# Copied patches written in four strips, images read in halves, and the second part of each group's patches read from GpSimd's queue

## What is computed

```python
xn   = (x - mean(x, (2, 3))) / sqrt(var(x, (2, 3)) + 1e-5)
pat  = patchify(pad(xn, to=40), 8)                  # 32*25 patches, 32 x 10 x 10
log  = pat.mean((2, 3)) @ Wg + bg
r    = one_hot(argmax(log), 8) * softmax(log)
y    = einsum('ne,encij->ncij', r, [relu(conv3x3(pat, Wexp[e]) + bexp[e]) for e in range(8)])
out  = x + unpatchify(y)[..., :32, :32]
```

## Time and profile before

| | before |
|---|---|
| median of three runs | 229.51 us (228.51 to 230.57) |
| the profiled execution's own time | 225.47 us |
| its span, first to last instruction | 223.7 us |
| busy: PE / PE weight load / DVE / ACT / POOL | 174.3 / 151.8 / 162.6 / 127.8 / 8.7 us |
| mean granted TensorE clock | 0.88 of full speed |
| SP's queue | 58,844 packets, 35.54 MB, 59.9% of 16 DMA engines |
| DMA packets under 512 bytes | 53,898 of 59,326 |
| instruction queue q8 | 44 packets, 0.72 MB |

### The profile page before, as it was taken

One profiled execution on the slowest core, in us unless ns is written; L12 is line 12 of the kernel. 1 busy time (PEld: TensorE's weight loads), 2 busy tenths in 40 slices (PEclk: granted clock), 3 DMA queues, 4 the chain that ended last, 5 costly groups with the idle time before them and its releaser, 6 DMA issues.

```text
span 223.7 us, 12210 instructions
## 1 busy us (share of the span) xinstructions
PE 174.3 (78%) x5652; PEld 151.8 (68%) x5652; DVE 162.6 (73%) x367; ACT 127.8 (57%) x239; POOL 8.7 (4%) x10
## 2 busy tenths in 40 slices
PE   0198769998599969898699749894999977997730
PEld 0038658887488858687597648784888866896730
DVE  4796997995997549975997619990799758078145
ACT  3235527594796319971996366571498587786000
POOL 7700000000000000000000000000000000000000
PEclk9999995699979976999699955999569999997995
DMA  6784975599369474958496836955795488001002
GB/s 224 180 240 108 220 173 218 133 211 273 133 130 233 131 278 108 214 155 317 94 216 170 312 84 140 254 191 186 169 232 225 123 173 210 6 6 71 32 3 94
DMA packets 59326, 37.28 MB, mean 167 GB/s; under 512 B 53898, under 2 KB 54794, under 8 KB 58378
## 3 DMA queue, kind: packets, MB, share of 16 engines
q1 hardware_dynamic: 58844, 35.54, 59.9%
q10 hardware_dynamic: 432, 0.97, 1.2%
HBM read 21.62 MB, written 14.43 MB: 161 GB/s over the span
## 4 chain that ended last, share of the span: by engine, by line
PE 50%; DMA 13%; DVE 13%; issue 10%; SPq 9%; ACT 4%; DVEq 0%
PE conv_bank L551 33%; PE chunk_bank L540 14%; SPq L213 8%; DMA windows<-WIND 6%; DMA XT<-x 5%; ACT XG L470 2%; DMA out<-XT 2%; DVE ROWS L324 2%; DVE STATS L297 1%; DVE XN L312 1%; DVE WS L398 1%; PE chunk_bank L525 1%; DVE XG L371 1%; ACT WS L465 1%; DVE BLK L384 1%
## 5 line engine op out<-in xcount | busy, mean ns | idle before, releaser
L551 PE MATMUL conv_bank<-XG,WS 97*32 97x64 f32 x4800 | 114.7, 248 | 27.2 <-issue 24.4
L551 PEld LDWEIGHTS conv_bank<-XG,WS 97*32 97x32 f32 x4800 | 98.2, 155 | 37.1 <-issue 28.7
L465 ACT COPY WS<-chunk_bank 97x500 f32<-97x500 f32 (+1 forms) x150 | 76.1, 566 | 24.3 <-PE chunk_bank L540 22.8
L540 PE MATMUL chunk_bank<-HOTT,WPF 128*128 128x100 bf16 x768 | 53.8, 225 | 2.5 <-ACT WS L465 1.0
L540 PEld LDWEIGHTS chunk_bank<-HOTT,WPF 128*128 128x128 bf16 x768 | 41.8, 107 | 9.6 <-issue 3.3
L470 ACT COPY XG<-XG 32x1400 f32<-32x1400 f32 (+1 forms) x48 | 41.3, 861 | 7.5 <-DMA XG<-windows 6.7
L378 DVE STREAM_TRANSPOSE YT<-conv_bank 128x320 f32<-128x320 f32 x40 | 19.9, 508 | 24.6 <-PE conv_bank L551 24.3
L371 DVE COPY XG<-XG 32x1400 f32<-32x1400 f32 (+1 forms) x32 | 18.1, 567 | 0.7
L384 DVE STREAM_TRANSPOSE BLK<-YT 128x1024 f32<-128x1024 f32 x8 | 17.3, 2167 | 0.1
L324 DVE TENSOR_REDUCE ROWS<-XN 128x165 f32<-128x1650 f32 x8 | 14.7, 1841 | 0.1
L297 DVE BATCH_NORM_STATS2 STATS<-XT 128x6 f32<-128x512 f32 x16 | 10.3, 681 | 5.4 <-DMA XT<-x 5.4
(11 more groups left out here) (41 smaller groups left out, 79.6 us busy)
## 6 DMA issues: line engine op xcount, KB each, us to landing
XG<-windows SPq DMA_DIRECT2D x64, 150.0 KB, 3.5
windows<-WIND SPq DMA_DIRECT2D x7, 1250.0 KB, 7.1
XG<-windows SPq DMA_DIRECT2D x64, 100.0 KB, 2.4
out<-XT SPq DMA_DIRECT2D x16, 256.0 KB, 3.5
XT<-x SPq DMA_DIRECT2D x7, 512.0 KB, 5.3
windows<-WIND SPq DMA_DIRECT2D x3, 250.0 KB, 3.3
XT<-x SPq DMA_DIRECT2D x2, 256.0 KB, 4.5
windows<-WIND SPq DMA_DIRECT2D x1, 500.0 KB, 5.7
```

What stands on the lines that cost most here:

```text
L465: nc.scalar.copy(to, source).then_inc(chunk_copied, 1)
L540: last = nc.tensor.matmul(chunk_bank[c % NCB][:, j * GN:(j + 1) * GN], wide(co, kx), HOTT[:], start=True, stop=True)
L551: last = nc.tensor.matmul(o, WS[g % 2][0:KC, kx * C:(kx + 1) * C, patch], taps, start=kx == 0, stop=kx == TAPS - 1)
```

## The change

Five edits, all in the issuing of transfers and the waits on them:

1. `write_windows(g)` now calls `write_strip(g, v)` for all four strips and every group: rows of 2000 bytes three times, and of 4000 bytes once, where one transfer had rows of 10,000. VectorE's four window copies of a group each signal `strip_ready` in place of one signal behind all of them.
2. `load_x` reads each image group in two halves (256 KB each).
3. `read_patches` on SP issues part 0 only (8 transfers). Part 1 is issued by GpSimd, in a loop over the groups at the end of its list, behind a wait for the written windows.
4. GpSimd's second subtraction of the weights also waits for `normalised`.
5. ScalarE loads its activation table before it issues the loads of constants and gates.

```diff
         def x_arrived(g):
-            return x_loaded[g % XB], 16 * (g // XB + (g % XB > 0))
+            return x_loaded[g % XB], 32 * (g // XB + (g % XB > 0))
         def writes_done(g):
-            return 16 * (KEEP + g)
+            return 16 * KEEP * (g + 1)
...
+        def read_part(queue, g, part):
+            u, (lo, hi) = g % 2, PART_LOTS[part]
+            if g > 1:
+                queue.wait_ge(conv_done, LOTS * (g - 2) + hi)
+            for b in range(GI):
+                some = slice(b * NP + lo * LOT, b * NP + hi * LOT)
+                for ky in (0, 2):
+                    queue.dma_start(XG[u][ky * C:(ky + 1) * C, some],
+                                    windows_dram[u].rearrange("(n j) w -> j n w", j=C)
+                                    [:, some, ky * WIN:ky * WIN + KROWS]
+                                    ).then_inc(part_loaded[u][part], 16)
...
             def load_x(g):
-                sp.dma_start(XT[g % XB][:], x_rows[g]).then_inc(x_loaded[g % XB], 16)
+                for h in range(2):
+                    half = slice(h * HALF, (h + 1) * HALF)
+                    sp.dma_start(XT[g % XB][:, half], x_rows[g][:, half]
+                                 ).then_inc(half_loaded[h] if g == 0 else x_loaded[g % XB], 16)
...
+            def write_strip(g, v):
+                u, last = g % 2, NP if v == KEEP - 1 else (v + 1) * NB
+                if g > 1 and v == 0:
                     for part in range(2):
                         sp.wait_ge(part_loaded[u][part], 16 * READS * (g // 2))
-                sp.dma_start(windows_dram[u].rearrange("(p k) w -> p (k w)", k=NP), WIND[:]
-                             ).then_inc(windows_written, 16)
+                sp.wait_ge(strip_ready, g * KEEP + v + 1)
+                sp.dma_start(windows_dram[u].rearrange("(p k) w -> p k w", k=NP)[:, v * NB:last, :],
...
+            def write_windows(g):
+                for v in range(KEEP):
+                    write_strip(g, v)
             def read_patches(g):
                 sp.wait_ge(windows_written, writes_done(g))
-                for part, (lo, hi) in enumerate(PART_LOTS):
...
+                read_part(sp, g, 0)
...
             for part in range(PARTS - 1):
                 pool.wait_ge(part_ready, part + 1)
+                if part == 1:
+                    pool.wait_ge(normalised, 1)
                 nc.gpsimd.tensor_tensor(W0, W0, WPART[:, part, :], ALU.subtract).then_inc(rest_ready, 1)
...
+            for g in range(GROUPS):
+                if g == 1:
+                    pool.wait_ge(wp_loaded, 16 * PARTS)
+                pool.wait_ge(windows_written, writes_done(g))
+                read_part(pool, g, 1)
...
             act.dma_start(W0, weights).then_inc(w_loaded, 16)
+            nc.scalar.preload_act_table_set("natural_log_exp_and_others")
             act.dma_start(CONST[:], consts).then_inc(const_loaded, 16)
             act.dma_start(GATE[:], gates).then_inc(gate_loaded, 16)
-            nc.scalar.preload_act_table_set("natural_log_exp_and_others")
```

More of the change, by code:

```diff
@@ L124, in build @@
         normalised = sem("normalised")
-        strip_ready, windows_ready, windows_written = sem("strip_ready"), sem("windows_ready"), sem("windows_written")
+        strip_ready, windows_written = sem("strip_ready"), sem("windows_written")
         share_ready = sem("share_ready")
@@ L152, in x_arrived @@
         def x_arrived(g):
-            return x_loaded[g % XB], 16 * (g // XB + (g % XB > 0))
-        def windows_copied(g):
-            return (windows_ready, g) if g > 0 else (strip_ready, KEEP)
+            return x_loaded[g % XB], 32 * (g // XB + (g % XB > 0))
         def writes_done(g):
-            return 16 * (KEEP + g)
+            return 16 * KEEP * (g + 1)
         def weights_of(g, c):
@@ L201, in write_strip @@
                              WIND[:, v * NB * WIN * WIN:last * WIN * WIN].rearrange("p (k w) -> p k w", w=WIN * WIN)
                              ).then_inc(windows_written, 16)
+            def write_windows(g):
+                for v in range(KEEP):
+                    write_strip(g, v)
             def read_patches(g):
-                u = g % 2
                 sp.wait_ge(windows_written, writes_done(g))
-                for part, (lo, hi) in enumerate(PART_LOTS):
[L208 to L216, removed]
+                read_part(sp, g, 0)
@@ L232, in set_ones @@
                 sp.dma_start(XG[u][TAPS * C:KC].rearrange("p n k -> p (n k)"), ones).then_inc(ones_set[u], 16)
-            for h in range(2):
-                sp.dma_start(XT[0][:, h * HALF:(h + 1) * HALF],
-                             x_rows[0][:, h * HALF:(h + 1) * HALF]).then_inc(half_loaded[h], 16)
+            load_x(0)
             set_ones(0)
@@ L240, in _ @@
             spread(1)
-            write_strip(0)
+            write_strip(0, 0)
             spread(2)
             for v in range(1, KEEP):
-                write_strip(v)
+                write_strip(0, v)
             read_patches(0)
@@ L309, in normalise @@
                 if g > 0:
-                    dve.wait_ge(*windows_copied(g - 1))
+                    dve.wait_ge(strip_ready, KEEP * g)
                 inside = bass.AP(XN, PITCH + 1, [[PITCH * PITCH, 128], [PITCH, H], [1, W]])
@@ L318, in windows @@
                 dve.wait_ge(windows_written, writes_done(g - 1))
-                for to, source in window_copies():
-                    last = nc.vector.tensor_copy(to, source)
-                last.then_inc(windows_ready, 1)
+                copies = window_copies()
+                for to, source in copies[:2]:
+                    nc.vector.tensor_copy(to, source)
+                for to, source in copies[2:]:
+                    nc.vector.tensor_copy(to, source).then_inc(strip_ready, 1)
             def sums(g):
```

4 lines of the change are left out of this document (removed).

## The result

The changed kernel is slower: 236.24 us as the median of 6 runs (233.61 to 237.06), beside 229.01 of the kernel before on the same chip. The ratio is 1.039, with a 95% interval of 1.033 to 1.045. The forecast was 225.0 with a range of 217 to 236, and faster as the likeliest side.

A forecast was written before the change was run, and what follows sets the result against it. PE was taken as the bound, 78% busy, with 24.4 us of issue gaps. Terms -0.5 + 1.5 - 1.5 - 5.0 + 1.0 = -4.5 took the profiled 225.47 us to 221.0, as median 225.0; range 217 to 236.

The forecast's parts named there:

- What bounds the kernel: Whole kernel: PE busiest, 174.3 us or 78% of the span, its largest idle entry 24.4 us of issue gaps.
- Group 0: Before ScalarE's first copy of part 1: GpSimd issuing at 1.3 us each and images sharing bandwidth cost +1.5 us (+1 to +10.7).
- later groups, part 1: Groups after group 0: GpSimd's 10.4 us of issuing a group, in a period of 24, mostly hides, even at 20.8.
- the prediction's three terms for the move: Part 1 delayed in group 0, +1.5 us; SP freed of its reads, -1.5; VectorE's copies hindered by GpSimd, +1.0.
- The other terms, -0.5 and -5.0: Quicker first normalisation at the kernel's start, -0.5 us; shorter PE issue gaps from writing windows in strips, -5.0 us.
- GpSimd is slow at issuing: Rival, group 0: 2.6 us per issue makes part 1 late, +10.7 us there, 234.2 us in all; decides from 1.9; 25%.
- Start, -0.5: Kernel start: first normalisation 0.82 us in place of 1.82, gates perhaps asked for 1.28 later; -0.5 us (-1.0 to +0.3).
- SP relieved, -1.5: Group 2: images load earlier, VectorE's 2.72 us wait vanishes, PE's next need moves up; -1.5 us (0 to -2.7).
- Strips, -5.0: Heads of groups 1 to 5: smaller, earlier window writes remove a third of PE's 14.6 us issue gaps; -5.0 us (0 to -14.6).
- VectorE beside GpSimd, +1.0: Seven groups: VectorE's early patch copies are slowed while GpSimd issues reads, mostly hidden under waiting; +1.0 us (0 to +7).
- the gaps stay: Rival, PE's issue gaps: they wander elsewhere or follow PE's own rate, so strips bring nothing; +0.5 us, 230.0; 22%.

The follow-up runs named there:

- Experiments 1: Changed kernel with part 1 of groups 0 and 1 back on SP: 229.03 us, ratio to the kernel before 1.010; timed again 229.47 us, 1.001.
- 2: Changed kernel, but GpSimd waits until part 0 of groups 0 and 1 has landed before asking for part 1: 227.93 us, ratio to before 1.011.
- experiment 5: Kernel before with single edits: first, part 1 moved to GpSimd, 235.35 us, ratio 1.034; strips only, 227.37, 0.992; start edits only, 228.31, 1.010.
- experiment 6: Changed kernel variants: GpSimd waits for part 0 in every group, ratio to before 1.016; GpSimd reads groups 4 to 7 only, 1.011 and 1.012; group 7 only, 0.992.
- Experiment 4: Changed kernel with both parts on SP, nothing issued by GpSimd: 226.18 us, ratio to before 0.985; second timing 225.08, 0.981; later 221.80 and 223.31.

## Why the prediction was wrong, step by step

**What bounds the kernel.** Right as far as it went: PE and its issue gaps. But the sentence "moving transfers helps PE only if these gaps hang on transfers" looked at one direction only. A transfer that no one waits for can be made one that is waited for.

**Group 0, the step that failed.** The prediction costed part 1 alone: GpSimd's price of one issue, and the bandwidth that the images would take from part 1. It set +1.5, with bounds set by the issue cost. That cost was over-estimated: 0.66 us each and not 1.3, and ScalarE's copy began at 33.03 against 32.31, +0.7. What it left out is part 0, which is needed first. In the kernel before the order of one queue protected it; with a second issuer the protection went, and VectorE's copy came 7.5 us later. In group 1, held to be hidden as "later groups, part 1", the same happened once more: 5.25 us of waiting by VectorE, 4.28 by PE. Its rows were there to be read: part 0 was copied at 25.72 with nothing waiting, and PE began behind it at 27.01 after 0.65 us, so that nothing was to spare: by half of SP's 8.73 us for 16 reads the earlier trace rows and 2.3 us of landing, part 0 was there at about 19.21 + 4.4 + 2.3 = 25.9. Experiments 1 and 2 show the cause by taking it away in two opposite ways, experiment 5 by setting it up alone. It is worth 6 to 9 us (ratios of 1.011, 1.010 and 1.001 in place of 1.039).

The whole move to GpSimd cost more than that. The changed kernel with both parts on SP has ratios of 0.975 to 0.985, the changed kernel 1.039: 5 to 6%, 12 to 15 us, against the +1.0 of the prediction's three terms for the move (+1.5, -1.5 and +1.0). What groups 0 and 1 don't explain of it is the open cost of experiment 6. The other terms, -0.5 and -5.0, weren't far off as a sum: with the halves, for which the prediction had no term, they measured -3.3 to -5.6 us.

**The rival on the other side.** "GpSimd is slow at issuing" had 25% and the right sign, with 234.2 near the result, but its mechanism is refuted: 0.66 us each is far below its deciding point of 1.9, and ScalarE's copy stayed well before 37. Its place, group 0, was right; it named the wrong part.

**Start, -0.5.** Nearly nothing in the trace, and no gain in its own run. The first normalisation fell to 0.81, as told, but VectorE then stood for the gates. Timeline of VectorE in the kernel after:

```profile
8.55 0.81 DVE L318 TENSOR_SCALAR XN<-XT,MV,RSTD 128x1024 f32<-128x1024 f32 x1
10.29 1.87 DVE L332 TENSOR_REDUCE ROWS<-XN 128x165 f32<-128x1650 f32 x1 [0.93 <-DMA GATE<-gates]
```

The sums began at 10.50 before, so 0.21 us is left of 1.00. The reason given for a loss was wrong. The gates were not asked for later. Timeline of ScalarE's queue and ScalarE in the kernel after:

```profile
1.17 1.28 ACT L482 ACT_TABLE_LOAD   x1 [1.17 <-PEq L658]
1.20 0.43 ACTq L483 DMA_DIRECT2D CONST<-consts  x1
1.67 0.45 ACTq L484 DMA_DIRECT2D GATE<-gates  x1
```

The queue issues beside the table load. The gates take 8.5 us to land in both kernels and arrive at about 10.2, which the slow normalisation had covered.

**SP relieved, -1.5.** The wait of 2.72 us in the earlier trace rows is gone as told: after, the statistics of group 3 begin at 90.23 without one. With the kernel 11 us behind by then its worth can't be read. Experiment 4 loses nothing by putting the reads back on SP, so the relief was not worth a measurable time.

**Strips, -5.0.** The sign was right and the size too large: alone they bring 0.8%, 1.7 us (0.3 to 3.2), together with the halves 1.5 to 2.5% of the time, 3.3 to 5.6 us. The mechanism isn't shown. With strips alone the issue gaps are 26.7 us against 24.4; with both parts on SP, strips and halves they are 21.9 and 19.0 (experiment 4, its first two profiles), but with neither strips nor halves, in the first kernel of experiment 5, they are 20.6. At the heads of groups 1 to 5, where the prediction wanted "near 10 and not 14.6", these first two have 8.1 and 5.9; what goes there comes back in part elsewhere. In the tail of the kernel after, where the DMA share is 0.12 (windows view below, last row), there is still one every 3.6 us; PE's timeline:

```profile
212.11 2.31 PE L559 MATMUL conv_bank<-XG,WS 97*32 97x64 f32 x127 [1.30 <-issue]
215.75 2.34 PE L559 MATMUL conv_bank<-XG,WS 97*32 97x64 f32 x128 [1.33 <-issue]
219.38 2.31 PE L559 MATMUL conv_bank<-XG,WS 97*32 97x64 f32 x127 [1.29 <-issue]
```

The counts in these rows say more about such gaps. From one of them to the next PE has 127 or 128 matmul records and as many of weight loads, 255 together, and one q8 packet arrives in each such stretch (DMA view, 209.5 to 213, 213 to 217 and 217 to 220). Over the kernel it is 11,304 PE records for 44 q8 packets, 257 each. So in this tail PE stands about 1.3 us for each block of instructions, with hardly a transfer beside it. Whether the gaps in the middle of the kernel are of the same kind isn't shown.

This speaks for the rival "the gaps stay" in the tail at least: a coincidence of gaps with the window write, read from one execution, was taken for half a cause.

**VectorE beside GpSimd, +1.0.** Too high, because the two hardly meet, and not because they don't hinder each other. In the kernel after VectorE's patch copies start at 33.24, 60.71, 83.24 and so on, and never lie beside GpSimd's issuing, which starts at 19.91, 47.93, 65.42, 88.21 and so on. So it says nothing that these copies take 567 ns in the mean in both kernels. One set of window copies does lie beside it. Timelines of VectorE, then of GpSimd, with a set that met nothing beside each:

```profile
41.88 1.19 DVE L329 COPY WIND<-XN 128x400 f32<-128x400 f32 x4
49.09 1.52 DVE L329 COPY WIND<-XN 128x400 f32<-128x400 f32 x4
...
47.93 5.75 POOL L184 DMA_DIRECT2D XG<-windows  x8 [22.65 <-DMA windows<-WIND]
65.42 5.21 POOL L184 DMA_DIRECT2D XG<-windows  x8 [11.73 <-DMA windows<-WIND]
```

VectorE loses 0.33 us and GpSimd 0.54; GpSimd's longest issue, 1153 ns in place of 658, is the one at 47.93, beside VectorE's normalisation at 48.03. In experiment 2, where GpSimd starts when part 0 lands, the patch copies do meet it: 2.41 and 2.48 us in place of 2.33, and 5.86 us for GpSimd's eight reads. This agrees in kind with the lock that the prediction named from the Trainium skill, "SBUF — State Buffer", section "SBUF: two separate sides". Its size here is some tenths of a microsecond at each meeting, far below the 8.8.

**The sum of what was seen**, from PE's waits in both profiles. Patches +11.9, issue gaps -4.6 (with one of 0.6 before L540), waits for ScalarE -3.1, the first one of all -1.1 (10.6 to 9.5), waits for VectorE's sums and selections +3.2: together +6.3. With PE's busy time, +2.8, this is 9.1 against the 8.8 measured. PE's longer busy time goes with a lower granted clock, 0.843 for the kernel against 0.880. Windows view, three stretches (busy us of PE, PEld, DVE, ACT, POOL; then granted clock, DMA share, GB/s), of the kernel after:

```profile
19.00:57.00 38.00, 27.78 (x770) 25.08 (x771) 26.90 (x64) 19.64 (x36) 11.12 (x16) 0.77 0.70 155
57.00:85.00 28.00, 22.45 (x678) 20.02 (x679) 21.07 (x48) 16.07 (x32) 5.21 (x8) 0.76 0.86 223
...
206.00:232.00 26.00, 12.89 (x679) 11.90 (x678) 13.73 (x22) 6.77 (x10) 0.00 (x0) 0.92 0.12 43
```

and of the kernel before:

```profile
19.00:57.00 38.00, 32.91 (x958) 29.49 (x956) 32.45 (x79) 21.51 (x42) 0.00 (x0) 0.87 0.79 204
57.00:85.00 28.00, 22.94 (x744) 20.16 (x747) 20.97 (x50) 17.48 (x33) 0.00 (x0) 0.87 0.64 165
```

The clock is lower in the two stretches in which PE stood 8.37 and 4.28 us, and the second takes 22.45 us of PE for 678 matmul records where it took 22.94 for 744 (the mix in it is not quite the same; a group's convolutions are 300 matmuls and 600 such records). So such a wait may cost more than its own length. That isn't shown: in the kernel of experiment 4 (second timing) the granted clock between 28 and 52 is 0.67, though PE stands for 3.0 us just ahead of it and for 1.9 us in it only.

## What to carry to other kernels

Before a transfer is moved to a second engine's queue, look at what the order of the one queue protects: ask which part is needed first, how much it has to spare (here under 1 us), and what it shares the DMA engines with afterwards. If the DMA engines are already busy for most of that stretch (here 79%), a second issuer changes who comes first and not how much arrives. What beats both kernels here is the change without its second queue: both parts on SP, the windows in strips and the images in halves, 1.5 to 2.5% faster in four timings.

## What was unexpected

- GpSimd issues a read of 480 rows in 0.66 us (64 of them, median and least both 658 ns), not far above the 0.46 that SP takes for 320 rows; but its transfers of 150 KB take 4.9 us to land in the median, where SP's took 3.5.
- ScalarE's queue issues transfers beside an activation table load: 1.20 against a load from 1.17 to 2.45.
- Reads on GpSimd's queue for which no engine waits cost 2.0 to 3.6% here when four or six groups have them, with a place in the trace that differs from run to run. Their cause wasn't found.
